# Splitting the row weighting of a fused up-sampling pass over both units of a chunk

## The reference, cut to what matters

```
up = jnp.repeat(pre_up, 2, axis=1) * w_up[None, :, None, None]
return _bilinear_up_x2(up) + sx                     # layer 0
...
xP = jnp.einsum('bcn,nk->bck', x2, P)               # P: 128*128 positions x 64 frequencies
...
out = jnp.einsum('bvk,bkn->bvn', WvxP, out / lamdv) # layer 1
out = out + out_bias
return gamma * out.reshape(Bb, Cc, Hh, Ww) + x
```

## Time and profile before

| what | value |
|---|---|
| runs | 3565.6, 3566.51, 3569.8 us; median 3566.51 us |
| profiled execution | 3571.49 us, span 3569.7 us |
| busy, share of the span | PE 88%, PEld 64%, DVE 80%, ACT 52%, POOL 40% |
| last pass | from about 1890 us to the end, 8 images |
| one middle image, 2517.4 to 2725.7 us | 208.3 us |
| the last image, 3347.9 to 3563.4 us | 215.5 us |

### The profile page before, as it was taken

How to read it: one execution, slowest core, us unless ns; L and a number is a source line. 1 busy time by engine, 2 the same in 40 slices (tenths; PEclk the granted TensorE clock), 3 DMA queues, 4 the chain that set the end, 5 groups by cost and what they waited for, 6 DMA issues and landing times. The chain is left out here.

```text
span 3569.7 us, 63832 instructions
## 1 busy us (share of the span) xinstructions
PE 3146.1 (88%) x23398; PEld 2281.7 (64%) x23398; DVE 2855.6 (80%) x3726; ACT 1866.9 (52%) x4385; POOL 1430.4 (40%) x805
## 2 busy tenths in 40 slices
PE   6999999999999969995867989899898988989777
PEld 3555555455554536652446878889787887978777
DVE  4999999899999872203556989888898988889887
ACT  4555555555555534241316656665666656566554
POOL 2676655666666550000002333333333333333333
PEclk9999999999999989596978989999998999999888
DMA  6665665556665634352035989999898999989897
GB/s 256 269 254 228 252 276 231 218 217 240 272 246 229 239 146 174 125 211 66 0 136 200 364 330 361 348 332 360 326 362 331 359 337 347 354 320 360 326 323 286
DMA packets 190891, 946.97 MB, mean 265 GB/s; under 512 B 13505, under 2 KB 13633, under 8 KB 170626
## 3 DMA queue, kind: packets, MB, share of 16 engines
q1 hardware_dynamic: 190594, 943.04, 69.9%
HBM read 638.90 MB, written 301.99 MB: 264 GB/s over the span
## 5 line engine op out<-in xcount | busy, mean ns | idle before, releaser
L1365 PE MATMUL second_o<-second_right,second_left 128*128 128x128 f32 x8192 | 1127.9, 289 | 207.3 <-POOL second_left L1146 126.7
L1146 POOL TENSOR_TENSOR second_left<-second_mid_copy,second_coef_rep 64x1024 f32<-64x1024 f32 x256 | 624.0, 2437 | 1610.9 <-ACT second_mid_copy L1472 1574.6
L1365 PEld LDWEIGHTS second_o<-second_right,second_left 128*128 128x128 f32 x8192 | 1043.5, 203 | 259.5 <-issue 235.8
L217 DVE SCALAR_TENSOR_TENSOR first_partial<-first_x,first_wd,first_partial 128x512 f32<-128x512 f32 (+3 forms) x1200 | 1045.5, 1005 | 0.0
L1607 DVE SCALAR_TENSOR_TENSOR second_x<-second_o,second_shift,second_x 128x512 f32<-128x512 f32 x1024 | 732.9, 739 | 203.5 <-PE second_o L1365 195.7
L290 ACT ACTIVATE first_xT<-first_tp 128x512 f32<-128x512 f32 x1024 | 610.2, 598 | 525.5 <-PE first_tp L317 524.7
L317 PE MATMUL first_tp<-all_const,first_x 128*128 128x128 f32 x4096 | 677.5, 289 | 68.3 <-ACT first_xT L290 36.1
L317 PEld LDWEIGHTS first_tp<-all_const,first_x 128*128 128x128 f32 x4096 | 436.5, 142 | 454.1 <-issue 403.7
L329 PE MATMUL first_freq<-first_xT,first_p 128*64 128x256 f32 x4096 | 668.5, 407 | 9.5
L197 POOL TENSOR_SCALAR first_product<-first_x,first_wd 128x512 f32<-128x512 f32 (+1 forms) x272 | 447.0, 1643 | 494.1 <-ACT first_acc L283 468.8
L1472 ACT ACTIVATE second_mid_copy<-second_mid_t 64x512 f32<-64x512 f32 x256 | 151.7, 593 | 485.0 <-PE second_mid_t L1335 481.6
(11 more groups left out here) (236 smaller groups left out, 2307.8 us busy)
## 6 DMA issues: line engine op xcount, KB each, us to landing
second_x<-in_x SPq DMA_DIRECT2D x256, 1024.0 KB, 11.0
out<-second_x SPq DMA_DIRECT2D x256, 1024.0 KB, 8.6
first_x<-in_x SPq DMA_DIRECT2D x48, 4224.0 KB, 24.6
first_x<-in_x SPq DMA_DIRECT2D x16, 4096.0 KB, 14.5
gather_d<-downsampled SPq DMA_DIRECT2D x24, 2048.0 KB, 12.6
downsampled<-first_acc SPq DMA_DIRECT2D x64, 512.0 KB, 3.5
second_dd<-downsampled SPq DMA_DIRECT2D x64, 512.0 KB, 12.5
first_p<-in_p_cols SPq DMA_DIRECT2D x1, 4096.0 KB
```

Source lines behind the costliest of these rows:

```text
L217: return nc.vector.scalar_tensor_tensor(out=after[:, rows, left:], in0=tap_window(xt[c], (s, dh, dw), count, row0), scalar=wd[:, t, weight ...
L1146: return eng.tensor_tensor(left[a][rows, odd:HALF:2, :, :].rearrange("p n (t s) g -> p n t s g", t=T), turned[rows, :, :, :].unsqueeze(3). ...
L1365: last = nc.tensor.matmul(ob[n][:, r, :], left[a][:, r, n, :], right[a][:, r, :], start=True, stop=True)
```

## The change

`weight` no longer gets e (which of two output rows of a pair) but r (0 for the eight multiplications into `mid`, 1 for the eight into `part`) and loops over e itself. ACT's `step` calls it once in every unit: `mid` of chunk m + 2 behind the copy in the even unit, `part` behind the copy in the odd unit. The wait for the loaded rows and for the free `mid` buffer goes with r = 0, the wait for `interpolated` (the `part` buffer has been read) with r = 1. `weighted` is raised behind the last multiplication into `part`, as before behind the sixteenth.

```
-                def weight(b, m, e):
+                def weight(b, m, r):
...
-                    if e == 0:
+                    if r == 0:
...
                         act.wait_ge(mid_turned, (b * CH2 + m) * 2 - 2 + TURN_LEAD)
-                        if m > 0:
-
-                            act.wait_ge(interpolated, b * CH2 + m)
-                    for r in range(2):
+                    elif m > 0:
+
+                        act.wait_ge(interpolated, b * CH2 + m)
+                    for e in range(2):
...
-                    if e == 1:
+                    if r == 1:
                         last.then_inc(weighted, 1)
...
-                        for e in range(2):
-                            weight(0, m, e)
+                        for r in range(2):
+                            weight(0, m, r)
...
-                    if u % 2 == 1 and (more or m + 2 < CH2):
-                        weight(b, m + 2, 0)
-                        weight(b, m + 2, 1)
+                    if more or m + 2 < CH2:
+                        weight(b, m + 2, u % 2)
```

## The result

The changed kernel takes 3387.27 us (median of 4 runs, 3385.43 to 3391.46), against 3568.16 us for the kernel before: a ratio of 0.9492 (95% interval 0.9477 to 0.9506), 181 us less. The forecast was 3446 us with a range down to 3400, so the sign and the places were right and the size too small. Its profiled execution took 3387.63 us. Lines of `kernel.py` behind `weight` are one lower than before (L1587 is the old L1588, L1606 the old L1607).

What follows compares the result with a forecast made beforehand. PE, DVE and DMA were near their limits in middle images, waits for POOL behind ACT's late copy set the last. Seven images' 86 us plus the last's 34.5 gave 120.5 us gained: 3446 us, range 3400 to 3508.

Steps and rivals of the forecast that it cites:

- The odd unit's copy: ACT's copy in odd units: its 2.5 us lateness goes; product to product shortens by 3.1 us.
- The even unit's copy: ACT's copy in even units: 2.52 us more stand before it, covered by 3.10 us idle; costed at nothing.
- The edge: Between images, before unit 1: eight fewer multiplications bring ACT's `place_vt` 2.5 us forward.
- three terms of waiting: PE's waits in a middle image: gains of 10.2 us for POOL, 2.5 for `place_vt`, 2.3 under "issue".
- The waits that move with r: ACT's waits for the `mid` buffer and `dd` rows: no cost, 0.5 us to spare in the worst case.
- The clock: PE's missing cycles, at most 8.3 us in a middle image and 28 in the last; 1.5 taken per middle image.
- DVE is busy for 185.8 of 191.8 us: DVE in a middle image, 97% busy, taken to allow at least 186 us.
- sum for a middle image: Gains of 16.5 us give 191.8 us if nobody else objects; 196 taken, from 208.3, for DVE and DMA.
- slower rival: L1588 and L1597 both meet POOL's instruction in every chunk, DVE carries 2.5 us more a chunk: 3684 us; chance 0.04.
- The DMA engines at today's time per packet: Transfers busy 198 us in a middle image and 181 in the last; 181 taken as the last image's bound.
- more than forecast: The clock comes back in full, at most another 7 us an image: below 3400 us; chance 0.08.
- The rule of about 358 GB/s a core: HBM limit on SBUF transfers: a middle image would stop at 202.5 us, the whole near 3501; doubted from the trace.

Runs made afterwards that it cites:

- lightened run: Changed kernel with half of the x rows not loaded after the first four chunks of the first image: 3380.43 us, ratio 0.9467 to the kernel before.
- the holding put back: Changed kernel with DVE's sum of mid and part moved from behind an even unit's third addition to behind the second: 3435.64 us, ratio 0.9619.

## Why the prediction was right in kind and too small

1. *The odd unit's copy* (part 1) held as written: lateness 0.04 us, POOL back to 2.36 us, waits for POOL 11.9 to 2.6 and 49.4 to 2.8.

2. *The even unit's copy* (part 2) held: 0.51 us of idle were left where 0.58 were worked out. Even twelve multiplications there cost no time, though those copies were 0.7 us late.

3. *The edge* (part 3) held roughly: an image's two waits for `place_vt` fell from 4.9 us (1.02 and 3.90; the 6.2 of the earlier trace rows holds a third, of the next image) to 3.0, by 1.9 where 2.5 were taken. The three terms of waiting were put at 10.2 + 2.5 + 2.3 = 15.0 us an image; PE's idle time fell by 11.0.

4. *The waits that move with r* (part 4) were put at nothing with 0.5 us to spare, from landing times of the slower kernel. In the changed one the longest landing of `dd` is 15.2 us instead of 14.1, and ACT waits twice, 3.8 us together. It is a small miss.

5. *The clock* (part 5) was a mis-sized term. I took 1.5 us of the 8.3 that the missing cycles bound; PE's busy time fell by 8.2 us an image, with a clock of 0.99 where it was 0.95. For the last image the bound of 28 was within the 165 us that the forecast's sum gave without a floor, and was then cut off by the floor of the transfers; the run with unused matmuls gives 31.5.

6. *DVE is busy for 185.8 of 191.8 us* (sum for a middle image) was wrong as a floor. That busy time held waiting: L1588 and L1597 fell from 1824 and 911 ns in the mean to 1342 and 675, 92 us in the pass, and DVE's busy time in a middle image is now 172.4. The earlier trace rows showed the least durations; I used them for a slower rival and not to take the holding out of the floor.

7. *The DMA engines at today's time per packet* (both sums) was the step that failed outright: a floor that is not there. I put 198 us into the choice of 196 for a middle image and took 181 for the last. The seven images take 188.6 us in the mean, and the last fell by 51.6, which makes 163.9 of the 215.5, next to the 165 of the sum without the floor. The lightened run shows no transfer on the path of a middle image. From the share of 0.95 at 348 GB/s to 1.00 at 382 the engines' busy time per byte fell by 4%, and from 0.84 at 304 to 1.02 at 414 by 11%; why it does is open. The 404 GB/s of a chunk in the earlier trace rows, which I called a burst, was nearer to what they sustain (414 in the last image).

The balance: the pass lost 134.5 + 51.6 = 186.1 us where 120.5 were forecast. Of the 65.6 that are missing, the floors took 29 in the seven images (191.8 to 196) and 16 in the last (165 to 181), and the clock's term 47 (7 times 6.7); the terms of waiting were too large by 28 (7 times 4.0). So the floor of the transfers and the clock failed by about the same, and the excess in the waits hid part of it.

The 4.2 us an image that I gave back for the floors of DVE and the transfers were not owed. The case above the forecast, "more than forecast", was the true one, since the clock came back nearly in full; I gave it 0.08. The rule of about 358 GB/s a core ("DMA: Bandwidth & Descriptors", section "Where 436 GB/s comes from", Trainium skill) did not bind this kernel on its one core: 382 GB/s over a middle image. The slower rival's mechanism is real, since the holding put back costs 48 us, but the new order moves out of it.

## What to carry to other kernels

Work of a middle engine that waits in one lump in front of a short hand-over is best split until each part fits the idle time before a hand-over; read that idle time from the timeline, and expect a plateau rather than an optimum (8 and 12 were equal here, since other limits took over). When a stall of PE goes, price its followers with it: the slow products behind it, and the busy time of other engines that was waiting in disguise. A busy share near 1 of the DMA engines need not be a floor; a run with part of the loads left out tells whether it is.

## What the runs showed of the hardware

- Unused matmuls in a PE stall made the kernel 0.9% faster (3541.82 us, ratio 0.9908) without a change in the order of the other work, with a granted clock of 0.99 instead of 0.87 in the last image.
- The 16 DMA engines moved 414 GB/s of mixed loads and stores over 162 us, at a share of 1.02; a share of 0.84 had gone with 304.
- Behind 3.40 us of idle PE the granted clock of the kernel before went to 0.50 until about 3416 us, and a product of 8 matmuls took 1.53 us instead of 1.13.
- DVE's sum of two SBUF inputs took between 1202 and 3379 ns for the same 128x1024 elements, by where POOL's instruction stood. Small instructions beside POOL's were stretched too: one of 64x64 elements from 269 to 2379 ns, a tensor_scalar of 64x128 from 272 to 2181.
- The last pass began between 1877.2 and 1898.9 us in executions whose earlier passes were the same program; differences of a few us between kernels are better read from image to image than from the whole.
